# Residual added by identity products on TensorE, squares in a buffer of their own

## The reference, cut to what matters

```python
x = x + _L0_conv_ref(_gn(x), w0, w1, w2, bias)   # 3 levels: Haar DWT, 5x5 conv over 4*32 channels, inverse DWT
x = x + _L1_conv_ref(_gn(x), spatial_weight)

# _L1_conv_ref(x, spatial_weight): patches = the 25 shifts of x in a zero-padded 5x5 window
dot = jnp.einsum('bchw,bckhw->bkhw', x, patches)
norm_x = jnp.sqrt(jnp.sum(x * x, axis=1))
norm_p = jnp.sqrt(jnp.sum(patches * patches, axis=1))
sim = dot / jnp.maximum(norm_x[:, None] * norm_p, EPS)
weight = (sim + 1.0) * 0.5 * spatial_weight[None, :, None, None]
out = jnp.einsum('bckhw,bkhw->bchw', patches, weight)
```

## Time and profile before

| | |
|---|---|
| median of 3 runs | 2223.08 us (2222.95 to 2223.33) |
| profiled execution | 2207.9 us, its span 2206.2 us |
| mean granted TensorE clock | 0.850 of full speed |
| busy: PE, DVE, ACT, POOL | 1613.0, 1406.8, 740.0, 448.3 us |
| DMA | 329.93 MB, mean 150 GB/s |

### The profile page before, as it was taken

The page is one execution under the profiler, slowest core; times in us unless marked ns, Lnnn a source line. Parts: engine busy times, 40 slices in busy tenths (PEclk is TensorE's granted clock), DMA queues, the critical chain, the costliest instruction groups (busy, mean ns, idle before and its releaser), DMA issues.

```text
span 2206.2 us, 49286 instructions
## 1 busy us (share of the span) xinstructions
PE 1613.0 (73%) x16895; PEld 853.4 (39%) x16895; DVE 1406.8 (64%) x2121; ACT 740.0 (34%) x1222; POOL 448.3 (20%) x792
## 2 busy tenths in 40 slices
PE   4776786778677786878668786878678786874465
PEld 3542343434333343434334343434334343432244
DVE  6427756866488456966478556966478445875354
ACT  2321243424243243423343243424243243423341
POOL 1343413012311213013311213012311113011000
PEclk8988997989888898979888897989888887987566
DMA  5243337673767547663766547673767448572665
GB/s 166 76 107 95 117 104 187 159 185 105 182 165 195 131 107 197 164 177 104 180 166 191 145 107 191 169 183 96 184 162 192 116 106 205 137 200 76 147 168 135
DMA packets 151105, 329.93 MB, mean 150 GB/s; under 512 B 47092, under 2 KB 96244, under 8 KB 150260
## 3 DMA queue, kind: packets, MB, share of 16 engines
q1 hardware_dynamic: 109296, 207.18, 36.9%
q0 software_dynamic: 41472, 118.24, 19.7%
HBM read 238.70 MB, written 86.61 MB: 147 GB/s over the span
## 4 chain that ended last, share of the span: by engine, by line
PE 29%; DMA 20%; SPq 19%; DVE 16%; issue 11%; ACT 3%; DVEq 1%; POOL 1%; ACTq 0%; POOLq 0%
DMA d_n<-st_n 11%; PE conv L1295 9%; DMA unit_mem<-d_n 8%; PE conv L1269 5%; SPq L410 5%; PE gram L1360 4%; SPq L384 4%; SPq L403 3%; PE out_ps L1382 3%; SPq L382 3%; PE conv L1254 2%; SPq L400 2%; PE stat_ps L1318 2%; DVE wgt L1017 2%; PE vals_ps L1343 2%
## 5 line engine op out<-in xcount | busy, mean ns | idle before, releaser
L1295 PE MATMUL conv<-thl,wconv 128*128 128x496 f16 (+2 forms) x1920 | 551.2, 417 | 23.9 <-DVE xa L896 12.5
L1017 DVE SCALAR_TENSOR_TENSOR wgt<-gram,tapw 124x512 f32<-124x512 f32 x512 | 350.0, 686 | 286.7 <-PE gram L1360 245.7
L468 POOL DMA_DIRECT2D ring<-in_x x576 | 333.7, 584 | 568.4 <-DVE bn L778 339.9
L1360 PE MATMUL gram<-unit_mem 128*60 128x128 f16 x4096 | 259.7, 253 | 221.9 <-DMA unit_mem<-d_n 128.2
L1360 PEld LDWEIGHTS gram<-unit_mem 128*60 128x60 f16 x4096 | 158.1, 117 | 444.8 <-issue 443.6
L1269 PE MATMUL conv<-thl,wconv 128*128 128x480 f16 (+7 forms) x1200 | 265.8, 377 | 0.0
L1295 PEld LDWEIGHTS conv<-thl,wconv 128*128 128x128 f16 x1920 | 169.4, 105 | 225.3 <-issue 73.2
L1318 PE MATMUL stat_ps<-st_n,sq_c 128*128 128x306 f32 x256 | 120.5, 560 | 170.0 <-ACT st_n L553 138.2
L1382 PE MATMUL out_ps<-wgt,vals 124*32 124x128 f32 x4096 | 194.6, 312 | 30.4 <-issue 24.4
L553 ACT ACTIVATE vals<-vals_ps 124x512 f32<-124x512 f32 x128 | 76.4, 597 | 363.3 <-PE vals_ps L1343 363.2
L1269 PEld LDWEIGHTS conv<-thl,wconv 128*128 128x128 f16 x1200 | 118.8, 101 | 132.0 <-issue 22.5
(11 more groups left out here) (133 smaller groups left out, 2057.8 us busy)
## 6 DMA issues: line engine op xcount, KB each, us to landing
unit_mem<-d_hl SPq DMA_DIRECT2D x128, 360.0 KB
unit_mem<-d_hl SPq DMA_DIRECT2D x256, 180.0 KB
ring<-in_x POOLq DMA_DIRECT2D x288, 128.0 KB, 3.3
ring<-in_x POOLq DMA_DIRECT2D x288, 127.0 KB, 3.6
d_hl<-st_hl SPq DMA_DIRECT2D x128, 180.0 KB
d_v<-st_v SPq DMA_DIRECT2D x128, 180.0 KB
unit_mem<-d_v SPq DMA_DIRECT2D x64, 360.0 KB
up<-d_z POOLq DMA_DIRECT2D x160, 128.0 KB, 3.2
```

The costliest lines, as they stand in the source:

```text
L468: pool.dma_start(dst, src).then_inc(raw_in[slot], 16)
L1017: V.scalar_tensor_tensor(out=dst, in0=g, scalar=SIM_SCALE ** 2, in1=tapw[:, :].unsqueeze(1).to_broadcast([KN, 2, 2 * QN]), op0=ALU.add, op ...
L1295: last = mm(dst[:, :, b0:b1], wconv0[:, w, 2 * (p % ROWS4) + s, dx + 2, :], thl[:, p % 2, d, s, :, b0 + dx:b1 + dx] if p % ROWS4 != 1 else ...
L1360: last = mm(bank[row:row + KQ, col:col + QN], key[:, q, e_at, TH * KW * g:TH * KW * g + KQ], tile[:, :, TH * g + 1:TH * g + 1 + TH, 1:1 + ...
```

## The change

The residual is no longer written to DRAM and read back. On TensorE, at slot 4 of stage j ahead of the unit's first values product, one product with a row of zeros opens the whole bank `out_ps`, and 16 fp32 products of x1's rows with 32 columns of the identity (scaled once by `unscale[0]`) put the residual into it; all products of the unit then accumulate, with `stop` at the last. The result is a copy with the mean as bias, on ScalarE, ahead of `vals_out`. Squares go to a buffer `st_sq` of their own; `half_in` waits for `unit_low` of half band h - 2 in place of the save, which `norms` now waits for. The values' high parts are made behind the norms, their low parts at slot 6 in place of slot 0. `finals` waits for the residual's products in place of the save of x1, and `set_live` for the results that read the old mean. SyncE's `load_residual` and GpSimd's `save_x1` go, with their calls.

```diff
@@ -180,11 +180,11 @@
...
-        x1_res = sb("x1_res", [P, Q, TH, H0], F32)
+        st_sq = sb("st_sq", [P, UN], F32)
+        zero_row = sb("zero_row", [1, P], F16)
...
@@ -410,17 +409,6 @@
-            def load_residual(b, r):
...
@@ -432,12 +420,10 @@
                for h in range(2):
                     save_half(b, h)
                     load_unit(b, h)
-                load_residual(b, 0)
                 save_half(b, 2)
                 for u in range(2 * BANDS):
                     if u % 2 == 0 and u > 0:
                         store_band(b, u // 2 - 1)
-                        load_residual(b, u // 2)
@@ -483,11 +469,6 @@
-            def save_x1(n, r):
...
@@ -593,11 +566,19 @@
-            def residual_in(b, r):
-                act.wait_ge(live_set, b + 2)
-                act.wait_ge(x1_res_in, 64 * (4 * b + r + 1))
-                part = x1_res[:, :, :, :].rearrange("p q h w -> p (q h w)")
-                copy(part, part, scale=unscale[0], bias=mean_ls).then_inc(res_ready, 1)
+            def result(b, u):
+
+                r, half = u // 2, u % 2
+                act.wait_ge(group_done, START + 4 * (8 * b + u + 1))
+                if u == 0:
+                    act.wait_ge(live_set, b + 2)
+                if half == 0:
+                    act.wait_ge(stored, START + 64 * (4 * b + r))
+                o = out_ps[:, :].rearrange("p (q h w) -> p q h w", q=Q, h=TH)
+                for rp in range(2):
+                    dst = ostage[:, rp:2 * TH:2, IMG // 2 * half:IMG // 2 * (half + 1)].rearrange("p h (w c) -> p c h w", c=2)
+                    last = copy(dst, o[:, 2 * rp:2 * rp + 2], bias=mean_ls)
+                last.then_inc(unit_out, 1)
@@ -623,17 +604,21 @@
-                act.wait_ge(half_saved[half], START + SAVES * (4 * b + h // 2))
+                act.wait_ge(unit_low, START + 8 * b + (h - 1 if h >= 2 else 0))
...
+
+            def square_half(b, h):
+
                 act.wait_ge(x2_done, 8 * b + h + 1)
-                part = st_x2[:, half, :, :].rearrange("p h w -> p (h w)")
-                copy(st_n[:, half, :], part, scale=1 / X_SCALE, func=ACT.Square).then_inc(sq_done, 1)
-                copy(in_strips(st_v[:, 0, half, :]), strips(part)).then_inc(v_high, 1)
+                if h > 0:
+                    act.wait_ge(n2_ready, 16 * b + 2 * h)
+                copy(st_sq[:, :], st_x2[:, h % 2, :, :].rearrange("p h w -> p (h w)"), scale=1 / X_SCALE, func=ACT.Square)\
+                    .then_inc(sq_done, 1)
 
             def norms(b, h, p):
@@ -641,6 +626,7 @@
 
                 if p == 0:
                     act.wait_ge(unit_vec, START + 8 * b + h)
+                    act.wait_ge(half_saved[h % 2], START + SAVES * (4 * b + h // 2))
                 copy(st_a[:, p * PIECE:(p + 1) * PIECE], stat_ps[:, 0:PIECE], func=ACT.Abs_reciprocal_sqrt,
                      bias=tiny[:, :])
                 copy(st_n[:, h % 2, p * PIECE:(p + 1) * PIECE], stat_ps[:, 0:PIECE]).then_inc(n2_kept, 1)
@@ -648,6 +634,7 @@
                     act.wait_ge(n2_kept, START + 16 * b + 2 * h + 2)
                     act.wait_ge(unit_low, START + 8 * b + h)
                     copy(st_b[:, :], st_a[:, :], func=ACT.Square).then_inc(root_squared, 1)
+                    copy(in_strips(st_v[:, 0, h % 2, :]), strips(st_x2[:, h % 2, :, :].rearrange("p h w -> p (h w)"))).then_inc(v_high, 1)
 
             def count_own(b, h):
@@ -677,6 +664,7 @@
                     half_in(b, 0)
+                    square_half(b, 0)
                     half_in(b, 1)
@@ -687,6 +675,7 @@
                     norms(b, 0, 0)
                     norms(b, 0, 1)
+                    square_half(b, 1)
                     count_own(b, 0)
                     unit_highs(b, 0)
@@ -702,11 +691,13 @@
+                    square_half(b, 2)
                     norms(b, 2, 0)
                     norms(b, 2, 1)
                     count_own(b, 2)
                     unit_highs(b, 2)
                     half_in(b, 3)
+                    square_half(b, 3)
                 for j in range(CONV_TILES):
                     if conv and j == 2:
@@ -715,6 +706,8 @@
                     if ls:
+                        if j > 0:
+                            result(b, j - 1)
                         vals_out(b, j, 0)
                     if ls and j + AHEAD < 2 * BANDS:
                         norms(b, j + AHEAD, 1)
@@ -728,11 +721,12 @@
                             unit_highs(b, j + AHEAD)
                         if j + AHEAD + 1 < 2 * BANDS:
                             half_in(b, j + AHEAD + 1)
-                        if j % 2 == 0:
-                            residual_in(b, j // 2)
+                            square_half(b, j + AHEAD + 1)
                     if conv and j in (5, 6):
                         for c in range(2 * (j - 5), 2 * (j - 4)):
                             fill(i + 1, c)
+                if ls:
+                    result(b, CONV_TILES - 1)
 
 
             for n in range(3):
@@ -779,6 +773,8 @@
 
             def set_live(i):
 
+                if not first(i):
+                    dve.wait_ge(unit_out, START + 8 * (i - 1))
                 V.tensor_copy(mean_ls, mean_conv).then_inc(live_set, 1)
                 dve.wait_ge(live_set, i + 1)
                 V.tensor_tensor(mean_conv, gn1[:, 2:3], biasq, ALU.add)
@@ -928,8 +924,7 @@
                 dve.wait_ge(acc_step, acc_count(n, 4 * half, SUMS_AT[3]))
                 if not first(n):
                     dve.wait_ge(x2_done, 8 * (n - 1) + 6 + 2 * half)
-                    for r in (2 * half, 2 * half + 1):
-                        dve.wait_ge(x1_saved[r], 16 * n)
+                    dve.wait_ge(res_read, 8 * (n - 1) + 4 + 4 * half)
                 s2 = sd[:, :, :, :].rearrange("p g s w -> p g (s w)")
                 row = H0 // 2 * half + 2 * pair
                 stt(two_rows(x1, row), s2, 1.0 if pair == 0 else 0.25, two_rows(xa, 2 + row)).then_inc(x1_done, 1)
@@ -1017,20 +1012,6 @@
-            def result(b, u):
...
@@ -1102,10 +1083,8 @@
                             weights(b, j, k, short_ones)
                             if k == 0 and j in (2, 3, 4, 5):
                                 pad_row(b, (6, 7, 0, 1)[j - 2])
-                            if k == 2 and j > 0:
-                                result(b, j - 1)
                             if h < 2 * BANDS:
-                                if k == 0:
+                                if k == 6:
                                     value_lows(b, h)
                                 if k == 3:
                                     units_open(b, h)
@@ -1229,6 +1205,9 @@
                         raw_stats(0, c)
             steps.link(dve, V.tensor_scalar(rel2, unscale[2], wscale[0], X_SCALE, ALU.mult, ALU.mult))
             V.tensor_scalar(rel1, unscale[1], wscale[0], 0.5 * X_SCALE, ALU.mult, ALU.mult)
+            dve.wait_ge(wlevel_mm, 6)
+            V.memset(zero_row[:, :], 0.0)
+            V.tensor_scalar(ident, ident, unscale[0], None, ALU.mult).then_inc(gain_set, 1)
             dve.wait_ge(wfull, TILES_ALL)
@@ -1315,7 +1294,7 @@
 
                 pe.wait_ge(n2_kept, START + 16 * b + 2 * h + p)
                 pe.wait_ge(flag_done, START + 8 * b + (h if h >= AHEAD else 0))
-                mm(stat_ps[:, 0:PIECE], same_quadrant, st_n[:, h % 2, p * PIECE:(p + 1) * PIECE], start=True, stop=True)\
+                mm(stat_ps[:, 0:PIECE], same_quadrant, st_sq[:, p * PIECE:(p + 1) * PIECE], start=True, stop=True)\
                     .then_inc(n2_ready, 1)
 
@@ -1370,17 +1349,31 @@
+            def residual(b, u):
+
+                r, half = u // 2, u % 2
+                pe.wait_ge(unit_out, START + 8 * b + u)
+                pe.wait_ge(x1_done, 4 * b + 4)
+                if u == 0:
+                    pe.wait_ge(gain_set, 1)
+                mm(out_ps[:, :], zero_row[:, :], wconv0[0:1, 0, 0, :, :].rearrange("p t o -> p (t o)")[:, 0:BANK], start=True, stop=False)
+                o = out_ps[:, :].rearrange("p (q n) -> p q n", q=Q)
+                for g in range(BANDS):
+                    row = BH * r + TH * g
+                    for q in range(Q):
+                        last = mm(o[C * g:C * g + C, q, :].rearrange("p (h w) -> p h w", h=TH), ident[:, C * q:C * q + C],
+                                  x1[:, row:row + TH, UW * half:UW * (half + 1)], start=False, stop=False)
+                last.then_inc(res_read, 1)
+
             def filter_group(b, u, e):
 
-                if e == 0:
-                    pe.wait_ge(unit_out, START + 8 * b + u)
                 pe.wait_ge(vals_done, START + 16 * b + 2 * u + e // 2 + 1)
                 pe.wait_ge(wgt_done, START + 8 * (8 * b + u) + 2 * e + 2)
                 o = out_ps[:, :].rearrange("p (q h w) -> p q h w", q=Q, h=TH)
                 for c in range(2):
                     for g in range(BANDS):
                         last = mm(o[C * g:C * g + C, :, :, TW * e:TW * e + TW], vals[:, (e * BANDS + g) * 2 + c, :],
```

(27 more changed lines are left out.)

15 lines of the change are left out of this document (removed).

## The result

The changed kernel takes 2238.47 us (median of 7 runs, 2226.59 to 2248.67), the kernel before 2218.92 us in runs on the same chip; the ratio is 1.0085, 95% interval 1.0048 to 1.0123. It is slower by a little under 1%, where the forecast was faster by 1.7% and its range ended at 2228. The profiled execution took 2231.0 us (span 2229.3) against 2207.9, at a mean granted clock of 0.885 against 0.850: the loss comes in spite of a higher clock.

What follows compares the result with a forecast made beforehand. Bound: a ring of half-band preparation, save, unit load and multiply, not one engine. Per pass -1.3 - 8.2 + 4.0 = -5.5, seven passes -38.5: profiled 2207.9 to 2169 us, median 2185; own range 2165 to 2205, 8-in-10 range 2145 to 2228.

Steps and rivals of the forecast that it cites:

- Stage 2 starts 8.2 us earlier: Start of stage 2: squares in their own buffer and fewer residual transfers bring it 8.2 us earlier; bounds 3 and 11.
- the loop edge: Between passes: VectorE's first sums come some 1.6 us earlier, so TensorE gains its 1.26 us wait; 1.3 us taken.
- 6 us or more: Test set beforehand: the prediction is wrong if stage 2 does not start at least this much earlier from the pass's start.
- a less crowded queue: Before stage 2: beyond the head's 5 us, faster issue of half band 3's save brings unit 2 about 8 us earlier.
- the ring hands the 8.2 us on: Stages 2 to 5: the two-stage loop of half-band saves and unit loads passes stage 2's 8.2 us gain along.
- R's delay in stages 2 and 4: Residual products delay VectorE's later slots and next save 1 us at most, set against 0.8 saved; VectorE is fuller.
- R = 2.0: Slot 4: residual products' TensorE time per unit, in us: 32 instructions 1.6, plus zero product; bounds 1.5 and 4.2.
- Stage 6 was to grow by 2.0: Stage 6: nothing covers one unit's residual products, 2.0 us; stages 6 and 7 together 4.0 per pass.
- rival (a): Residual products fully side by side, stage 6 perhaps at higher clock: -9 to -12 us per pass, 2139 to 2158; chance 0.2.
- rival (d): Waits for squares stay because another condition comes as late, residual products are paid: +19 us, 2242; chance 0.05.
- (c): Residual products run in order (3.5 us), seen in stages 2, 4, 6, 7: +4.5 per pass, 2255; chance 0.15.
- Rival (b): ScalarE waits at the norm read as long as at the copy, stage 2 gains 3 us: 2221; chance 0.12.

Runs made afterwards that it cites:

- run 5: Changed kernel without the residual's 16 products in units 2 and 4 (output lacks the residual there): ratio 0.9949 to the kernel before.
- run 4: Changed kernel without the residual's 16 products in every unit, the zero product kept (output lacks the residual): ratio 0.9789 to the kernel before.
- runs 7 and 8: GpSimd's last level-1 load and eight raw-image loads held until unit 6 has landed: in the changed kernel 0.9898, in the kernel before 0.9893, both to the kernel before.
- run 3: Changed kernel with the residual's products reordered, quadrant outer and band inner, so neighbours go to different column groups: ratio 0.9944 to the kernel before.
- q_order: Kernel of run 3: the changed kernel with the residual's products ordered quadrant outer, band inner; ratio 0.9944 to the kernel before.

## Why the prediction was wrong

The forecast was -5.5 us per pass. The five passes show +3.3. By the steps of the prediction:

- **Stage 2 starts 8.2 us earlier, and the loop edge gives 1.3: together 4.8.** By the prediction's own sign, 6 us or more, it was wrong here. (The wait of 1.26 us is gone, but it stood behind the pass's first product, so the table counts it here; ahead of that product TensorE idles 3.2 us in the mean in place of 3.4.) The head gained what was forecast: save 3's release came 5.2 us earlier, save 2 landed 3.0 us earlier, the waits for squares fell below 50 us, and the new wait stands in stage 1's slot 2 (4.95 us at 871.10). Stage 1 starts 5.4 us earlier and gives 0.6 back. What failed is the further 3 us that I gave to a less crowded queue. Load 2 was issued 9.9 us after save 3 (9.1 before) and took 17.1 us to land (15.9 before), so it landed 3.0 us earlier; stage 2 gained 4.8, as it starts 1.0 us behind the landing, not 2.7. The gain is not of the squares alone: alone they gave 1.5, the residual's part alone 1.2, together 4.8, and no run explains the rest. The error is 4.7 us.
- **Stages 2 to 5, "the ring hands the 8.2 us on": to stage 4 yes** (4.0 of 4.8, an error of 0.8), **then no.** The step that failed most is the sentence that sets R's delay in stages 2 and 4 to 1 us at most against 0.8 saved, because VectorE is the fuller engine. It failed in stage 4; of stage 2 nothing shows (run 5). The residual stands in slot 4 ahead of gram products that VectorE needs next; VectorE waits there, and low 7 comes 23.8 us after stage 4's start, not 20.7: 3.1 us. Most of the rest is unit 6's landing, 22.9 us after issue, not 20.4: stage 5 starts 3.6 us earlier (183.8 for 187.4), and GpSimd's raw loads with it, while load 6, which follows low 7, moves by 0.5 only. I had not looked at what else is in flight when load 6 is. Together 5.6 us. Runs 4 and 5 show that these go with the residual, runs 7 and 8 what the collision takes of them.
- **R = 2.0: 2.8.** The zero product, with the allowance of 0.15 for a tile change that no row showed, took 0.32 us to the next start where I had 0.41. A convolution product of 512 columns starts 0.22 us after the last (the trace's median), so 0.10 is what the row of zeros, with its change of tile, took on top. The 32 products took 2.46 where I took 1.6, between rows of 1.3 and 3.5. The reason given for the middle, "neighbours change group here only after four", was the right worry and too small. In stage 7 it cost 2.6 us (14.6 to 17.2), 0.6 more than forecast.
- **Stage 6 was to grow by 2.0 and shrank by 0.7.** Most of its low clock fell into the wait ahead of it (below). This is 2.7 us in my favour, and luck: the prediction says nothing of it outside rival (a).
- **Last pass, 0: a gain.** From the start of the last pass with convolutions to the end it is 444.7 us, before 449.5; with +3.3 in the first of those two passes, the last one gained about 8.

4.7 + 0.8 + 5.6 + 0.6 - 2.7 - 0.2 (the idle ahead of a pass's first product) = 8.8 us per pass, the distance from -5.5 to +3.3. Times seven that is 62 us. The 8 us of the last pass are given back by set-up (1.1) and the first of the seven passes (262.3 us against 252.0, 7 more than 3.3): 62 again, from the forecast 2169 to the profiled 2231.

By the number rival (d) came nearest, 2242 for 2238.5, but by chance: the waits for squares did go, from 138.2 to 33.7 us. By the mechanism it is (c), though its 2255 is further off. Its place was right for stages 4, 6 and 7 (for stage 2 nothing shows), and R is at its point of decision, 2.8. Its strict order at 3.5 us did not come, as the 32 took 2.46; and it hung on the same gain of 8.2. Rival (b), where the wait only moves, describes what the squares did alone.

## What to carry to other kernels

Ask of every stage what ends it, not what waits in it: the norm wait of 8 us in stage 1 was real, and yet moving it gave 0.3% and taking away the wait for the save behind it another 0.5%, both at the edge of the noise, since the unit's load ended that stage anyway. Work added to an engine that is not the fullest can still cost its full length when a fuller engine waits for what comes behind it in the same stage (3.5 us of stage 4 for products of 2.46, run 4), and when the chain goes on through a queue. Ask too what else is in flight: a transfer that moves against another can collide with it more (unit 6's load took 20.4 us, then 22.9). In a queue that issues in order, put a transfer whose inputs are ready ahead of one that still waits: that exchange was worth four times the loss of the change. With the products in the better order the change is worth 0.6% (run 3); with the queue's orders and the held loads in both kernels, 3.4%.

## What the runs showed of the hardware

*The next column group started three instructions early, not eight.* In `q_order` four products of four column groups start 7 ns apart (884.609, .616, .622, .629), and the next four 0.11 to 0.13 us later. In the changed kernel, with eight instructions of one group in a row, each follows 0.11 us after the last (the group is read from this rhythm, as the trace does not name it), and the next group's first starts at 899.764, between the fifth (899.758) and the sixth (899.867) of the group before it: two groups run at once, not four. These starts are not in program order: group 1's first overtakes three instructions of group 0 (899.867, .976 and 900.086). But the overtaking has a reach, three instructions here: the 32 take 2.46 us in this order and 1.08 in the other.

*A longer wait was not followed by a longer stretch of low clock.* After 5.86 us of idle the products of the kernel before ran at a granted clock of 0.50 from 970 to 982 us; after 13.46 us of idle those of the changed kernel were back at 1.00 by 989.4, 4.5 us after the wait. In the two traces the clock is 0.50 from 968.5 to 982.1 us before and from 975.2 to 988.9 in the changed kernel. Of the second stretch 9.6 us lie in the wait, where there are no products to slow, and of the first 1.4. Four convolution products take 1.88 us at 0.50 and 1.02 at 1.00; the kernel before, then the changed kernel:

```profile
970.42 1.88 PE L1295 MATMUL conv<-thl,wconv 128*128 128x512 f16 x4
...
979.47 1.89 PE L1295 MATMUL conv<-thl,wconv 128*128 128x504 f16 x4
```

```profile
985.44 1.88 PE L1274 MATMUL conv<-thl,wconv 128*128 128x512 f16 x4
...
989.42 1.02 PE L1274 MATMUL conv<-thl,wconv 128*128 128x496 f16 x4
```

TensorE had done the same kind of work ahead of both waits, with the granted clock at 0.50 from 944.6 to 954.8 us in the kernel before (a wait of 3.10 us ends in there too) and at 1.00 for all of stage 5's products in the changed one. Over all seven passes it is alike: the changed kernel waits 11.4 to 13.5 us ahead of stage 6, and the stage's mean granted clock is 0.88 to 0.90; the kernel before waits 2.8 to 12.7 us, and it is 0.71 to 0.88. No run here varied the wait alone.
